# Neighbour sums of 48 x tiles on VectorE, ahead of each tile's product, in place of GpSimd

## The reference

```python
lap_x = left - 2*y + right            # along channels, reflect padding
lap_y = up   - 2*y + down             # along tokens, reflect padding
Y = zX*lap_x + zY*lap_y + zR*y*(1-y)  # the stencil, one zX, zY, zR per batch
h = Y @ W1.T + scale * Y @ m1.T + b1  # W1 2048x512, m1 a product of Y's rows 1..16
h = gelu(h)
out = h @ W2.T + scale * h @ m2.T + b2
x + out
```

## Time and profile before

| | |
|---|---|
| median of 3 runs | 1343.32 us (1342.73 to 1345.28) |
| the profiled execution | 1342.11 us, its span 1340.4 us |
| TensorE busy | 1333.8 us |
| VectorE busy | 1027.7 us |
| ScalarE busy | 789.4 us |
| GpSimd busy | 388.6 us |
| granted TensorE clock | 0.999 of full speed |

### The profile page before, as it was taken

One profiled execution on the slowest core, in us unless ns is written; L12 is line 12 of the kernel. 1 busy time (PEld: TensorE's weight loads), 2 busy tenths in 40 slices (PEclk: granted clock), 3 DMA queues, 4 the chain that ended last, 5 costly groups with the idle time before them and its releaser, 6 DMA issues.

```text
span 1340.4 us, 17071 instructions
## 1 busy us (share of the span) xinstructions
PE 1333.8 (100%) x5878; PEld 1100.1 (82%) x5878; DVE 1027.7 (77%) x1665; ACT 789.4 (59%) x1370; POOL 388.6 (29%) x368
## 2 busy tenths in 40 slices
PE   9999999999999999999999999999999999999998
PEld 7888887888888888888888888888878888888887
DVE  8888799958898688966889668896789967665343
ACT  6644566645675466664667546675466754566432
POOL 1013254502443023530245312542134510232000
PEclk9999999999999999999999999999999999999999
DMA  7764378777777677875778767686767866667661
GB/s 243 194 154 151 64 209 214 200 209 209 183 208 193 199 208 194 207 199 191 205 191 224 183 212 201 191 215 182 223 173 203 212 182 207 160 192 164 172 195 48
DMA packets 140070, 253.52 MB, mean 189 GB/s; under 512 B 13648, under 2 KB 37456, under 8 KB 139984
## 3 DMA queue, kind: packets, MB, share of 16 engines
q1 hardware_dynamic: 122032, 201.43, 46.8%
q0 software_dynamic: 17376, 49.29, 22.3%
q10 hardware_dynamic: 576, 1.72, 0.3%
HBM read 189.34 MB, written 63.05 MB: 188 GB/s over the span
## 4 chain that ended last, share of the span: by engine, by line
PE 91%; DVE 6%; issue 1%; ACT 1%; DMA 1%; POOL 0%; DVEq 0%; ACTq 0%; POOLq 0%
PE po L650 16%; PE po L648 16%; PE po L649 16%; PE ph L632 14%; PE ph L636 14%; PE ph L634 14%; DVE yl L1266 1%; DVE W2s L1294 1%; DVE y L1284 0%; DVE gl L1351 0%; DVE W2l L1302 0%; DVE y L1280 0%; DVE y L1254 0%; DVE y L1249 0%; PE po L604 0%
## 5 line engine op out<-in xcount | busy, mean ns | idle before, releaser
L648 PE MATMUL po<-W2h,gh 128*128 128x512 f32 x1020 | 396.8, 389 | 0.0
L650 PE MATMUL po<-W2h,gl 128*128 128x512 f32 x1020 | 396.8, 389 | 0.0
L649 PE MATMUL po<-W2l,gh 128*128 128x512 f32 x1020 | 396.8, 389 | 0.0
L632 PE MATMUL ph<-yh,W1h 128*128 128x512 f32 x896 | 349.1, 390 | 1.8 <-DVE ph L1336 1.4
L634 PE MATMUL ph<-yl,W1h 128*128 128x512 f32 x896 | 348.6, 389 | 0.0
L636 PE MATMUL ph<-yh,W1l 128*128 128x512 f32 x896 | 348.6, 389 | 0.0
L650 PEld LDWEIGHTS po<-W2h,gl 128*128 128x128 f32 x1020 | 191.5, 188 | 39.7
L649 PEld LDWEIGHTS po<-W2l,gh 128*128 128x128 f32 x1020 | 191.5, 188 | 39.8
L648 PEld LDWEIGHTS po<-W2h,gh 128*128 128x128 f32 x1020 | 191.5, 188 | 39.6
L632 PEld LDWEIGHTS ph<-yh,W1h 128*128 128x128 f32 x896 | 168.2, 188 | 38.8 <-DVE ph L1336 2.4
L636 PEld LDWEIGHTS ph<-yh,W1l 128*128 128x128 f32 x896 | 168.2, 188 | 34.9
(11 more groups left out here) (120 smaller groups left out, 1464.8 us busy)
## 6 DMA issues: line engine op xcount, KB each, us to landing
W2s<-in_w_dram SPq DMA_DIRECT2D x124, 256.0 KB, 3.3
R<-in_w_dram POOLq DMA_DIRECT2D x62, 512.0 KB, 7.5
uv_scratch<-UVs SPq DMA_DIRECT2D x112, 256.0 KB, 4.5
UVs<-uv_scratch SPq DMA_DIRECT2D x112, 256.0 KB, 3.7
X<-in_xT_dram SPq DMA_DIRECT2D x56, 390.0 KB, 4.5
xr<-in_x_dram SPq DMA_DIRECT2D x16, 1024.0 KB, 5.5
xr<-in_b_dram POOLq DMA_DIRECT2D x16, 1024.0 KB, 10.4
out_dram<-xr SPq DMA_DIRECT2D x64, 256.0 KB, 2.5
```

What stands on the lines that cost most here:

```text
L632: e.matmul(bank[:, :], W1h[:, f, blk, wc], yh[:, q, c, :], start=first and c == 0, stop=False, skip_group_check=not first)
L648: e.matmul(po[t][:, :], gh[:, lt, st], W2h[:, k, :], start=i == 0 and lt == 0, stop=False)
L649: e.matmul(po[t][:, :], gh[:, lt, st], W2l[:, k, :], start=False, stop=False)
L650: return e.matmul(po[t][:, :], gl[:, lt, st], W2h[:, k, :], start=False, stop=i == NI - 1 and lt == 1)
```

## The change

For the tiles of batches 2 to 7 (48 tiles) the calls of `side` and `token` leave GpSimd's list. VectorE gets a function `sums` with the same two additions into the same buffers, which waits for the x tile and for the tile before, and is called directly in front of each `mul`. Batch 1's eight tiles stay with GpSimd. Nothing else is changed.

```diff
--- before.py
+++ after.py
@@ -564,10 +564,6 @@
             top1(1, 0)
             top3(1, 0)
             add_b2(0, 1)
-            side(2, 0)
-            token(2, 0)
-            side(2, 1)
-            token(2, 1)
             for b in range(1, B):
                 for i in range(7):
                     top0(b, i + 1)
@@ -575,20 +571,10 @@
                     if i < 6:
                         add_W1(b, i + 2)
                     top3(b, i + 1)
-                    if b + 1 < B and i < 6:
-                        side(b + 1, i + 2)
-                        token(b + 1, i + 2)
                 add_b2(b, 0)
-                if b + 2 < B:
-                    side(b + 2, 0)
                 add_b2(b, 1)
-                if b + 2 < B:
-                    token(b + 2, 0)
                 if b + 1 < B:
                     add_W1(b + 1, 0)
-                    if b + 2 < B:
-                        side(b + 2, 1)
-                        token(b + 2, 1)
                     top0(b + 1, 0)
                     top1(b + 1, 0)
                     top3(b + 1, 0)
@@ -1204,6 +1190,15 @@
                 e.tensor_tensor(sd, up, down, ALU.add).then_inc(s_md, 1)
                 e.tensor_tensor(st, left, right, ALU.add).then_inc(s_mt, 1)
 
+            def sums(b, n):
+                mid, up, down, left, right = x_at(b, n)
+                st, sd = sums_at(b, n)
+                e.wait_ge(*x_done(b, n))
+                pb, pn = (b, n - 1) if n else (b - 1, 7)
+                e.wait_ge(s_tile, at_tile(pb, pn))
+                e.tensor_tensor(sd, up, down, ALU.add).then_inc(s_md, 1)
+                e.tensor_tensor(st, left, right, ALU.add).then_inc(s_mt, 1)
+
             def tile0(n):
                 e.wait_ge(s_sten, n + 1)
                 if n == 0:
@@ -1474,6 +1469,7 @@
                     part_l(1, 4)
             glL(0, 1, 6)
             w1lB(1, 0)
+            sums(2, 0)
             mul(2, 0)
             fin(2, 0)
             fold(1, 4, 0, 4)
@@ -1481,6 +1477,7 @@
             w1lT(1, 0)
             tile(2, 0)
             w2l(1, 4)
+            sums(2, 1)
             mul(2, 1)
             fin(2, 1)
             tile(2, 1)
@@ -1510,6 +1507,7 @@
                         w2l(b, 2 * i + 4)
                     fold(b, 2 * i + 5, 0, 1)
                     if nxt:
+                        sums(b + 1, i + 2)
                         mul(b + 1, i + 2)
                     fold(b, 2 * i + 5, 1, 4)
                     w1lT(b, i + 1)
@@ -1606,6 +1604,7 @@
                     if nxt and i < 7:
                         fold(b + 1, i - 3, 3, 4)
                     if i in (4, 6) and nxt2:
+                        sums(b + 2, (i - 4) // 2)
                         mul(b + 2, (i - 4) // 2)
             c21(B - 1, 7)
             glL(B - 1, 1, 7)
```

## The result

The changed kernel takes **1340.64 us** (median of 16 runs, 1339.66 to 1341.43), the kernel before 1343.2 us in the same comparison (16 runs, 1341.91 to 1345.28): a ratio of 0.998, with a 95% interval of 0.9973 to 0.9986. That is 2.6 us less, against 2.8 to 2.9 forecast: about 0.2%, and the interval leaves out no change. The profiled execution took 1341.16 us with a span of 1339.4; its clock was granted at 0.999.

A forecast was written before the change was run, and what follows sets the result against it. TensorE, busy 1333.8 of 1340.4 us, was taken to bound the kernel. Four stalls worth 2.8 us off the median of 1343.32 gave 1340.5, stated as 1340.4, with a range of 1338.6 to 1343.6.

The forecast's parts named there:

- The four stalls: TensorE's waits inside the loops, two on VectorE's L1336 and two on ScalarE's L913: 2.8 us together, expected to go.
- c22 stalls: TensorE's two waits on VectorE's L1336, 1.48 and 0.43 us lost, traced to token sums held back by `add_b2`.
- Batch 1's two waits on copies: TensorE's waits on ScalarE's copy L913, 0.42 and 0.45 us lost, traced to `part_l` taking 4.42 us beside GpSimd.
- the border that the prediction set: Time dividing faster from same: 1340.6 us, from a measurement that can tell about 0.2%, 2.7 us.
- The folds' relief: First-half steps: four folds on VectorE fall from 2.04 to 1.13 us without GpSimd's sums beside them, 0.91 us back.
- The sums' cost and the cycle: VectorE's first-half step: sums add 1.22 us a tile, cycle goes from 11.90 to 12.02 us, below TensorE's 12.24.
- idle time ahead of `mul`: VectorE's first-half step: 0.19 us idle ahead of `mul`, waiting for ScalarE, is covered by the sums.
- The backlog: VectorE in batch 3's first half: 0.56 us late behind step 1's folds and sums, growing to 0.95 in step 5.
- The fin of step 0: Batch 3 on VectorE: fin begins near 526.5 and ends near 528.1 instead of 527.9; tile 0.25 us late.
- Rival C: VectorE's first-half cycle passes TensorE's 12.24 us, as sums meet GpSimd or relief fails: 1359 or 1358 us; chance 0.09.
- Busy times: VectorE busy about 1037 us, 59 added and 50 returned, 36 first-half tiles giving 0.91 each; GpSimd at 264.
- No cushion I read is under 1.0 us: Argument against rival B, stalls traded for others (about 1342.7 us, chance 0.22); smallest spare read 1.03 us, at copy L913.

The follow-up runs named there:

- first_half_only: Changed kernel, but only tiles 2 to 7 have their sums on VectorE; tiles 0 and 1 stay with GpSimd: 1341.5 us, ratio 0.9991 to the kernel before.
- token_early: Kernel before with only GpSimd's order changed: token(b+2, 0) right behind side(b+2, 0), ahead of add_b2(b, 1): 1341.53 us, ratio 0.9992.
- second_half_only: Changed kernel, but only tiles 0 and 1 have their sums on VectorE; tiles 2 to 7 stay with GpSimd: 1341.56 us, ratio 0.9991 to the kernel before.
- both_engines: Changed kernel with GpSimd's 96 additions kept too; VectorE waits for them and writes the same sums again: 1362.66 us, ratio 1.0146 to the kernel before.

## Why the prediction was right

**What bounds it.** The four stalls were priced at 2.8 us and traced to GpSimd's additions. All four are gone in the changed kernel. Of the c22 stalls, one is back in first_half_only, where the token sum of the second half is GpSimd's again, and none is left in token_early, where that sum runs earlier. Batch 1's two waits on copies are both there in token_early, where nothing is taken from GpSimd, one of them in second_half_only, and none in first_half_only. The forecast of 1340.4 was 0.24 us under the measured median. That it is so close is in part luck. The 2.8 us were read off one execution in which batch 0 lost nothing at 107, and between the two profiled executions the span fell by 1.0 us only. The median fits the sum if the kernel before loses in batch 0 as well in most of its runs, as token_early did with the same code there, and as its median, 1.1 us above its profiled execution, would have it; no second profile of it shows that. By the border that the prediction set, 1340.6, the median lies just on the side of "same", to which it gave 0.39, against 0.49 for faster.

**The folds' relief.** Forecast 0.91 us a step, measured 0.91 to 0.92. Rule and row: the Trainium skill, SBUF — State Buffer, section Who interferes with whom, has a VectorE instruction with two SBUF inputs and a GpSimd instruction that reads SBUF exclude each other. The trace agrees in direction. In size, what the folds lost is less than the whole overlap (0.91 beside 1.09).

**The sums' cost and the cycle.** Forecast 12.02, measured 11.90. Two terms of the sum were mis-sized a little. The sums cost 0.60 us each by starts, not 0.61; and the idle time ahead of `mul` that it covers was 0.28 us by starts, not the 0.19 of the bracket: before, the fold ahead of `mul` began at 546.50 and lets the next instruction begin 0.26 us later, at 546.76, while `mul` began at 547.04. 11.90 - 0.91 + 1.20 - 0.28 = 11.91.

**The backlog.** The matmul that began at 548.52 begins at 549.53 in the changed kernel's execution, so batch 3 is compared with 1.01 us taken off. The fin of step 0, with its clock as recorded:

```profile
527.75 1.18 DVE L1249 SCALAR_TENSOR_TENSOR y<-SS,PK,y 128x512 f32<-128x512 f32 x1
...
529.46 0.73 DVE L1255 SCALAR_TENSOR_TENSOR y<-SS,PK,y 128x512 f32<-128x512 f32 x1
```

It begins at 526.74 by before's clock (forecast 526.5) and ends at 527.92 (forecast 528.1); tile begins at 528.45, at the same moment as before, where 0.25 us late was forecast. Step 1 leaves a backlog of 0.28 us (its sums take 1.20, its folds give back 0.92): the next folds begin at 544.36, which is 543.35 by before's clock, against 543.07. The forecast was 0.56. In the later steps, with a cycle of 11.90 as before, it stays at 0.28, where growth to 0.95 was forecast. The smallest spare at the copy L913 (L899 after) is 1.66 us (1.03 before), at `glE` 2.26 (2.54 before).

**Rival C** (the sums meet GpSimd) happened once, at the entry of batch 1, where the tops stand beside them. Timeline of VectorE:

```profile
186.73 1.23 DVE L1199 TENSOR_TENSOR SS<-X 128x512 f32<-128x512 f32 x1
187.88 1.69 DVE L1200 TENSOR_TENSOR SS<-X 128x512 f32<-128x512 f32 x1
```

GpSimd there:

```profile
186.34 1.07 POOL L533 TENSOR_TENSOR Ts<-Ts,R 128x256 f32<-128x256 f32 x1
...
187.96 1.05 POOL L537 TENSOR_TENSOR Ts<-Ts,R 128x256 f32<-128x256 f32 x1
```

2.77 us for a pair that costs 1.20. Its price per step was as computed: both_engines, which has the relief of the steps removed, gave 12.82 (forecast 12.93) and 0.53 us at a stall. What kept C away in the steps is distance: the top L537 ends at 542.7 in the step shown, the sums begin at 547.14.

**Busy times.** VectorE 1036.4 (forecast 1037): 59.4 added and 51 back, against 59 and 50. The division of the 50 was off: in a first half five groups of four folds were long before (those from 530.31 to 578.94 in batch 3), so 30 tiles returned it there, not 36. GpSimd 273.3 (264). The forecast took 124 us away. The records of its sums fell by 122.7 (76.7 + 68.0 before, 11.5 + 10.5 after), as the eight tiles that it keeps are its slow ones; but 7.4 of these had overlapped other records of GpSimd, which busy time counts once, so it fell by 115.3 only.

**What I missed** is batch 0's stall. "No cushion I read is under 1.0 us" did not cover batch 0: before had 0.37 us to spare there. Which instruction of VectorE stands beside GpSimd's two sums near 84 us, `w2l` or `part_l`, differs between executions by some tenths of a microsecond: before, `w2l` began 0.71 us ahead of the side sum and took 0.68 us; in the nine others it began at most 0.44 us ahead and took over 3 us. It is in the changed kernel's profiled execution and in its second one, so part of the expected 2.8 us is not in the span.

**Open.** How the 2.6 us divide among the parts: each half of the change gives 0.9 us by medians, with ratios whose intervals reach 1. The spread of before's runs (2.8 to 6.0 us in four comparisons) against 1.8 and 2.1 us for the changed kernel fits stalls that hang on when a transfer lands, but that was argued, not tried.

## What to carry to other kernels

Before an addition is given to an idle engine, look at what the busy engine does beside it: here 1.2 us of VectorE work a tile stood with GpSimd, and 0.91 us of it came back as longer folds in a step, with stalls of 0.4 to 1.5 us where GpSimd's sums met a long or an urgent instruction. Compare the cycle of an engine from one instruction to its next copy with that of the engine that bounds the kernel, by starts: that difference alone told within 0.05 us what a step lost in three kernels. And a place without a stall in one execution is safe only by the spare time that it shows: here 0.37 us was too little, since a collision that fell on `w2l` in place of `part_l` held up a load as well.

## What the runs showed of the hardware

- Four folds of 128 columns beside 1.09 us of one GpSimd addition took 2.04 us, not 1.13; `part_l` beside three GpSimd additions in a row took 4.42 us, not 1.22; `w2l`, 512 columns, beside two in a row took 3.62 us, not 0.68. Where GpSimd's instructions follow one another with no gap, the one of VectorE waits through several.
- It goes both ways: before, GpSimd's side sum took 1.28 us at the least and 2.24 at the most, its token sum 1.03 and 2.02, by their 56 records each. The longest of each, at 172.75 and 174.96, stood beside a 1,024-column sum of VectorE with two inputs (L1280).
- Two-input fp32 additions of 512 columns follow one another every 0.60 us on VectorE, while each record is 0.68 us long.
- A wait of TensorE costs more than its bracket shows: for 0.25 us idle at 587.19 the starts are 0.64 us apart, and 0.34 behind it, where 0.227 each is the pitch: 0.53 us in all.
